# Layer-zero product at the head of the turn, and halves of the squares exchanged by transfers inside SBUF

## What is computed

```
x = _layernorm(x + _L0_gnn_ref(x, adj, L0_gnn_bias))     # similarity graph over the 512 columns
x = _layernorm(x + _L1_gnn_ref(x, adj, W_lang, W_grav, W_V, W_O, gate_logit, log_sigma))
x = _layernorm(x + _L2_gnn_ref(x, adj, L2_gnn_bias))     # similarity graph again
x = _layernorm(x + _L3_gnn_ref(x, adj, adj, L3_gnn_bias))
```

## Time and profile before

| what | value |
|---|---|
| time, median of 3 runs | 1690.02 us (1685.96 to 1690.75) |
| profiled execution: its own time | 1692.68 us |
| profiled execution: its span | 1690.8 us |
| TensorE busy | 1510.8 us, 89% |
| VectorE busy | 1245.2 us, 74% |
| ScalarE busy | 993.8 us, 59% |
| GpSimd busy | 637.9 us, 38% |
| `gnn_layer_pair` within the span | from about 318 to 1181 us |

### The profile page before, as it was taken

How to read it: one execution, slowest core, us unless ns; L and a number is a source line. 1 busy time by engine, 2 the same in 40 slices (tenths; PEclk the granted TensorE clock), 3 DMA queues, 4 the chain that set the end, 5 groups by cost and what they waited for, 6 DMA issues and landing times. The chain is left out here.

```text
span 1690.8 us, 27935 instructions
## 1 busy us (share of the span) xinstructions
PE 1510.8 (89%) x7672; PEld 1239.3 (73%) x7672; DVE 1245.2 (74%) x3177; ACT 993.8 (59%) x1715; POOL 637.9 (38%) x814
## 2 busy tenths in 40 slices
PE   6899999599999999999999999983799881999997
PEld 4677887487878887878877878862688881777774
DVE  5788799547776667776667776653677898699997
ACT  7775455236656666557666557654333780577775
POOL 5553001013234443334443334433000000799997
PEclk9999999699999999999999999996899995899998
DMA  5320493212111222112221112000541000344442
GB/s 213 103 85 1 176 379 143 87 51 70 62 38 61 68 75 68 56 37 68 68 75 68 44 50 68 31 26 26 205 144 57 0 0 0 119 149 140 146 143 106
DMA packets 80627, 148.19 MB, mean 88 GB/s; under 512 B 8448, under 2 KB 8576, under 8 KB 80576
## 3 DMA queue, kind: packets, MB, share of 16 engines
q1 hardware_dynamic: 80576, 147.56, 25.4%
HBM read 97.06 MB, written 50.46 MB: 87 GB/s over the span
## 5 line engine op out<-in xcount | busy, mean ns | idle before, releaser
L814 POOL TENSOR_TENSOR rs_a<-ve_a,neghalf 128x1 f32<-128x1 f32 x64 | 35.6, 556 | 375.1 <-DVE nm_a L808 375.1
L226 PE MATMUL bank<-xn_lo,xn_hi 128*128 128x512 f32 (+1 forms) x640 | 145.3, 358 | 5.3 <-DVE xn_lo L203 5.1
L198 ACT ACTIVATE xn_hi<-xn 128x512 fp32r<-128x512 f32 x128 | 80.6, 630 | 117.3 <-DVE xn L191 117.2
L1710 POOL TENSOR_TENSOR xw_lo<-xres,xw_hi 128x512 fp32r<-128x512 f32 x64 | 83.1, 1299 | 131.6 <-ACT xw_hi L1675 131.6
L226 PEld LDWEIGHTS bank<-xn_lo,xn_hi 128*128 128x128 f32 x640 | 102.5, 192 | 19.3 <-DVE xn_lo L203 10.3
L1649 PE MATMUL l_ps<-an_hi,xw_hi 128*128 128x512 f32 x256 | 105.6, 413 | 10.0 <-POOL xw_lo L1710 8.7
L217 PEld LDWEIGHTS bank<-xn_hi 128*128 128x128 f32 x512 | 95.7, 192 | 24.4 <-ACT xn_hi L198 7.7
L322 POOL TENSOR_TENSOR sq_lo<-sq,sq_hi 128x512 fp32r<-128x512 f32 x64 | 87.3, 1382 | 60.9 <-ACT sq_hi L289 60.8
L959 PE MATMUL l_ps<-an_hi,xw_hi 128*128 128x512 f32 x256 | 102.2, 399 | 8.8 <-DVE xw_lo L1340 8.4
L536 DVE MATCH_REPLACE8 work<-best,work 128x520 f32<-128x520 f32 x160 | 108.3, 684 | 0.0
L203 DVE TENSOR_TENSOR xn_lo<-xn,xn_hi 128x512 fp32r<-128x512 f32 x128 | 105.8, 827 | 0.6 <-ACT xn_hi L198 0.4
(11 more groups left out here) (242 smaller groups left out, 4742.1 us busy)
## 6 DMA issues: line engine op xcount, KB each, us to landing
xr<-in_x SPq DMA_DIRECT2D x32, 512.0 KB, 3.3
xw_dram<-stage SPq DMA_DIRECT2D x64, 256.0 KB, 5.6
stage<-xw_dram SPq DMA_DIRECT2D x64, 256.0 KB, 2.6
stage<-in_x SPq DMA_DIRECT2D x64, 256.0 KB, 2.6
between<-xo SPq DMA_DIRECT2D x64, 256.0 KB, 2.0
xres<-between SPq DMA_DIRECT2D x32, 512.0 KB, 3.7
xin<-between SPq DMA_DIRECT2D x64, 256.0 KB, 2.7
out<-xo SPq DMA_DIRECT2D x64, 256.0 KB, 2.0
```

What stands on the lines that cost most here:

```text
L226: mm = self.nc.tensor.matmul(out, h[:, c * P:(c + 1) * P], l[:, a:b], start=(i == 0 and c != 1), stop=False, skip_group_check=True)
L1710: nc.gpsimd.tensor_tensor(xw_lo[:, i % 2, :], of_batch(ga, i), xw_hi[:, i % 2, :].bitcast(F32), ALU.subtract).then_inc(xw_lo_ok, 1)
```

## The change

TensorE begins a turn with `l0(0)` and does `yprod(0)` after it; `l0(1)` comes directly behind `k_turned`, and `yprod(1)` between the pairs of `l1`. So that `l0(0)` can start, `xw_hi_(0)` and `xw_lo_(0)` of the following group are made at the end of the turn in front (ACT: behind `exp_g`; DVE: behind `kernel_g`, ahead of `ht_lo(3)`). `turns` passes the following group to each engine, and one more turn at the end is written out, so that the loop has 13 passes in place of 14. ACT scales the first kernel matrix in place of DVE; the small coefficient operations are put together. ACT no longer writes `sq_turned`: SP copies the two halves of `sq` by two transfers for each batch, eight in a turn, and POOL's `fold(i)` waits for them. ACT's `high(2)` and `high(3)` move behind `scale_l`, and POOL's order is another one.

```
+            def exchange(gp, i):
+                sp.wait_ge(sq_ok, GRP * gp + i + 1)
+                sp.dma_start(sq_turned[0:HALF, i, :], sq[HALF:P, i, :]).then_inc(exchanged[i], 16)
+                sp.dma_start(sq_turned[HALF:P, i, :], sq[0:HALF, i, :]).then_inc(exchanged[i], 16)
...
-                                ("store", 2), ("store", 3), ("load", 1), ("load", 2), ("next", 1), ("load", 3)):
+                                ("swap", 0), ("swap", 1), ("store", 2), ("store", 3), ("load", 1), ("load", 2),
+                                ("next", 1), ("load", 3), ("swap", 2), ("swap", 3)):
...
+                if A:
+                    l0(0)
                 if B:
                     yprod(0)
-                if A:
-                    l0(0)
                 if C:
                     k_turned()
-                if B:
-                    yprod(1)
+                if A:
+                    l0(1)
                 if C:
                     l1(0)
                     l1(1)
-                if A:
-                    l0(1)
+                if B:
+                    yprod(1)
...
+                def kernel_l_scaled():
+                    act.wait_ge(cf_ok, gp + 1)
+                    for i in range(GRP):
+                        nc.scalar.activation(k_l[:, i, :], k_l[:, i, :], ACT.Identity,
+                                             scale=small[:, 4, i:i + 1]).then_inc(ka_ok, 1)
...
-                    nc.scalar.activation(sq[:, i, :], xo[:, i, :], ACT.Square)
-                    nc.scalar.activation(sq_turned[0:HALF, i, :], xo[HALF:P, i, :], ACT.Square)
-                    nc.scalar.activation(sq_turned[HALF:P, i, :], xo[0:HALF, i, :], ACT.Square).then_inc(sq_ok, 1)
+                    nc.scalar.activation(sq[:, i, :], xo[:, i, :], ACT.Square).then_inc(sq_ok, 1)
...
                 if C:
-                    for i in range(GRP):
-                        high(i)
+                    high(0)
+                    high(1)
...
                     scale_l()
+                if C:
+                    high(2)
+                    high(3)
+                if B:
                     v_hi(2)
                 if A:
                     ht_hi(2)
                 if B:
                     exp_g()
+                if following is not None:
+                    xw_hi_(0, following)
...
                 def fold(i):
-                    pool.wait_ge(sq_ok, GRP * gp + i + 1)
+                    pool.wait_ge(exchanged[i], 32 * (gp + 1))
...
                 keep(2)
+                keep(3)
+                root_a(3)
                 if gp is not None:
                     fold(2)
                     fold(3)
-                keep(3)
-                if gp is not None:
                     sq_lo(0)
                     sq_lo(1)
-                root_a(3)
+                if g is not None:
+                    pool.wait_ge(q_ok, g + 1)
+                    nc.gpsimd.tensor_tensor(r_l[:], q_l[:], s.neghalf[:], ALU.pow).then_inc(r_ok, 1)
                 if gp is not None:
                     sq_lo(2)
                     sq_lo(3)
-                if g is not None:
-                    pool.wait_ge(q_ok, g + 1)
-                    nc.gpsimd.tensor_tensor(r_l[:], q_l[:], s.neghalf[:], ALU.pow).then_inc(r_ok, 1)
...
                     kernel_l()
                     kernel_g()
+                if following is not None:
+                    xw_lo_(0, following)
                 if A:
                     ht_lo(3)
```

More of the change, by code:

```diff
@@ L875, in gnn_layer_pair @@
         stored = [sem(f"stored{i}") for i in range(GRP)]
+        exchanged = [sem(f"exchanged{i}") for i in range(GRP)]
         passed = sem("passed")
@@ L879, in turns @@
         def turns(eng, turn):
[L881 to L886, removed]
+            turn(None, None, 0, 1)
+            turn(None, 0, 1, 2)
+            with eng.Fori(0, groups - 3) as gp:
+                turn(gp, gp + 1, gp + 2, gp + 3)
+            turn(groups - 3, groups - 2, groups - 1, None)
+            turn(groups - 2, groups - 1, None, None)
+            turn(groups - 1, None, None, None)
         @block.sync
@@ L918, in turn @@
                         store(at, i)
+                    elif kind == "swap" and gp is not None:
+                        exchange(gp, i)
                 if gp is not None:
@@ L935, in _, with turn @@
         def _(pe):
-            def turn(gp, g, ga):
+            def turn(gp, g, ga, following):
                 def hturn(i):
@@ L1209, in turn @@
                     y_hi(1)
+                if A:
+                    xw_hi_(2)
                 if C:
@@ L1213, in turn @@
                 if A:
-                    xw_hi_(2)
                     norm_a(0)
+                if B:
+                    y_hi(2)
                 if C:
@@ L1218, in turn @@
                     square(1)
+                if A:
+                    xw_hi_(3)
+                if C:
                     norm_b(2)
                     norm_b(3)
-                if B:
-                    y_hi(2)
                 if A:
                     norm_a(1)
+                if B:
+                    y_hi(3)
                 if C:
@@ L1345, in ht_lo, with xw_lo_ @@
                     lo_part(ht[1][:, :, i, :], ht_ps[i % 2][:].rearrange("p (c n) -> p c n", c=CH), ht[0][:, :, i, :], ht_lo_ok)
-                def xw_lo_(i):
+                def xw_lo_(i, ga=ga):
                     dve.wait_ge(xw_hi_ok, GRP * ga + i + 1)
@@ L1427, in kernel_l_scaled @@
                                                    in1=small[:, 2, :], op0=ALU.mult, op1=ALU.mult).then_inc(cf_ok, 1)
[L1428 to L1431, removed]
+                    nc.vector.tensor_scalar(small[:, 5, :], small[:, 3, :], s.w_g[:, 0:1], None, ALU.mult).then_inc(sg_ok, 1)
                 def kernel_sum():
[L1435 to L1442, removed]
+                    dve.wait_ge(sg_ok, gp + 1)
                     for i in range(GRP):
@@ L1478, in turn @@
                         ht_lo(i)
+                    xw_lo_(0, following)
                     return
+                if C:
+                    coefficients()
                 if A:
-                    xw_lo_(0)
+                    xw_lo_(1)
                 if C:
-                    kernel_l_scaled()
                     kernel_sum()
+                if A:
+                    residual_a(0)
                 if B:
                     y_lo(0)
-                if A:
-                    residual_a(0)
-                    xw_lo_(1)
                 if C:
@@ L1498, in turn @@
                     residual_b(1)
-                    stats_b(0)
-                    stats_b(1)
                 if A:
                     residual_a(1)
+                if B:
+                    y_lo(1)
                 if C:
@@ L1507, in turn @@
                     xw_lo_(2)
+                if C:
+                    stats_b(0)
+                    stats_b(1)
+                if B:
+                    y_lo(2)
+                if A:
+                    xw_lo_(3)
                     stats_a(1)
@@ L1516, in turn @@
                     stats_a(2)
-                    xw_lo_(3)
                 if B:
```

25 lines of the change are left out of this document (9 added, 16 removed).

## The result

The changed kernel takes 1723.78 us (median of four runs, 1721.78 to 1724.5) against 1688.8 beside it: a ratio of 1.021, 95% interval 1.019 to 1.022. The forecast was 1716.0 within 1688 to 1728. The profiled execution has a span of 1721.5 us, 30.7 more than before. From `k_turned` of turn 2 to that of turn 16, in TensorE's timeline, the 14 full turns take 745.45 us against 713.73: +31.7, all of the loss.

The account below looks back on a forecast made before the run. TensorE was taken as the bound, busy 49.86 of 51.0 us a turn. Fourteen turns at +1.91 (26.7) and edges -0.7 gave +26.0 on the profiled 1692.7, or 1718.7; on the median 1716.0, range 1688 to 1728.

Parts of the forecast that it names:

- The collision: VectorE's diagonals, two SBUF operands, wait for GpSimd's running fold and squares; end 2.55 us later, turn 1.91 longer.
- The exchange's landing: Second half issued at offset 33.4, landing at 35.4 to 36.0; fold(2) taken to start at 35.8.
- the collision with turns taken: Main case: diagonals and GpSimd operations alternate on the shared port; 1708 to 1724 us, chance 0.50.
- the exchange lands late: Rival: each microsecond fold(2) comes later lengthens the turn by one; 1730 us, chance 0.10 together with a lower clock.
- The clock: TensorE's clock may fall behind the 2 us wait in hturn(2); late exchange or lower clock, chance 0.10.
- the third rival: Exchange lands late or TensorE's clock falls; one such microsecond makes +14, 1730 us; chance 0.10.
- `k_turned`: TensorE's wait there goes, as coefficient, scalings and sums end by 3.6 us, before 4.2: 0.79 us a turn gained.
- the prediction counts three: Last three diagonals beside GpSimd's r_l: the port rule would cost about 0.7 us a turn; forecast that they pass.
- The edges: Turns outside the full ones: turn 1 +1.2, turn 2's start -0.6, turn 16 -2.2, turn 17 +0.9; sum -0.7 us.
- No collision, 1678.3: Rival: diagonals don't wait for GpSimd, or only briefly; a turn gains 0.64, total 1678.3 us; chance 0.18.
- The 0.75 for `high(2)` and `high(3)`: Placed behind scale_l on ScalarE, they start v_hi(2) 0.75 us later, all of it reaching the head of the turn.
- This alone is worth nothing: Removing ScalarE's eight second squares, 0.63 us each a turn, gains nothing in a full turn; TensorE's work covers them.

Follow-up runs that it names:

- m_from_psum: Changed kernel, with the eight diagonals on VectorE reading m from its PSUM bank, only the identity from SBUF: 1691.94 us, 1.002 of the kernel before.
- before_two_dummies: Kernel before, plus two 128x512 additions of constants on GpSimd ahead of r_l in turns 2 to 16, starting with the diagonals: 1715.76 us, 1.016.
- m_psum_high_late: Changed kernel, diagonals reading m from PSUM and ScalarE's high(2), high(3) moved from ahead of v_hi(2) to behind ht_hi(2): 1682.03 us, 0.996 of before.

## Why the prediction was right, point by point

*The collision* was right in place, mechanism and price: one wait for each GpSimd operation, the sides taking turns, 1.1 us a wait; two runs show it with nothing else changed, *m_from_psum* (-32 us) and *before_two_dummies* (+27 us). *The exchange's landing* was mis-sized: 35.8 was taken for `fold(2)`, 638.21 - 601.50 = 36.7 came, as issues took 0.47 to 0.60 and not 0.45, and the landing 2.9 and not about 2.4. So the first diagonal waits for nearly all of `fold(3)`: three waits, not two, an end at offset 43.1 for 42.7, and a turn of +2.37 for +1.91. In the 12 turns 3 to 14 that is 5.5 us, about the 5 by which the full turns exceed the sum (31.7 for 26.7). The other two are not like them: from `k_turned` to `k_turned` turn 2 lost 3.07 and turn 15 only 0.16. Turn 15 has no load in front of the exchange: its `swap(2)` is issued at offset 30.5 in place of 32.6, `fold(2)` starts at 34.2, and one diagonal waits. So 1723.78 is the upper end of the 1708 to 1724 given to the collision with turns taken, and a part of the rival *the exchange lands late* came with it: the range held, the forecast of 1716.0 was 8 us short.

*The clock* fell behind most of the waits in `hturn(2)`, as the third rival had it, but TensorE's slow matmuls took the place of a wait for VectorE. *`k_turned`* is reached without a wait, as said. Only two diagonals start behind `r_l` in the turn shown (644.12 and 644.35), where the prediction counts three; neither waited. *The edges*: turn 1, with the earlier start of turn 2, +0.4 for 1.2 - 0.6 (71.24 against 70.83 from the stage's first matmul to the first of turn 2); turn 16 -2.0 for -2.2 (48.31 against 50.34 from its first matmul to the next turn's), its 2.52 gone; turn 17 +2.3 for +0.9 (25.52 against 23.20 from `k_turned` to `squares`), the exchange having no cover.

*No collision, 1678.3*: this rival's size was wrong by 14 us (*m_from_psum*, 1691.94, turn 51.26 for 50.38). Its turn left out two waits. `r_l` comes behind `sq_lo(1)`: in the turn shown it ends at offset 42.75, and `scale_l` starts 0.44 later than `a_l` would have let it. With `fold(2)` at 35.8, as forecast, `r_l` would have been in time (42.75 - 0.9, an estimate), so this is the mis-sized landing again. `q_l`'s wait beside the row was not in the sum at all. The turn with the first wait alone took 50.88; how the mean's 0.88 divides between the two was not measured by an edit. The 0.75 for `high(2)` and `high(3)` was right (0.73).

*"This alone is worth nothing"*, of ScalarE's second squares, fell: in the new order, without the collision, they cost 1.44 us a turn. The work named as cover, TensorE's, does not cover them, as `v_hi(0)` and `m_out` stand behind them, and with `m_out` begins the chain for whose end TensorE waits. Under the collision it hardly showed (53.66 against 53.43): the diagonals began 2.1 us later and waited once in place of three times, and ended at the same offset.

## What to carry to other kernels

Before moving work on GpSimd, list what VectorE runs in the new window: operations with two SBUF operands, and some with one, can stand still for up to a whole GpSimd operation of 1.27 us each, so that a 0.3 us operation costs 1.3. (Beside the 128x4 `r_l` they did not.) Reading one operand from PSUM, or putting a dependency between the GpSimd operations so that they keep away, cost nothing here and gave back 29 to 32 of the 35 us. When such a delay is taken out, price again what stood behind it: the gains of an exchange and of an order depend on what else is late, and here each showed only when the next was mended.

## What the runs showed of the hardware

A VectorE operation with a single SBUF source can wait too: `q_l` (a 128x4 `tensor_scalar`, 0.16 us alone) took up to 1.30, and the 128x512 clamp of `a_g`, 0.43 alone, took in *m_psum_high_late* (min/median/max):

```profile
L1429 DVE TENSOR_SCALAR a_g<-a_g x16: 429/842/956, 383.5 to 1133.9; 128x512 f32<-128x512 f32 x16
```

The Trainium skill ("SBUF — State Buffer", section "SBUF: two separate sides") has the shared port taken by VectorE operations in a two-port mode as well as by those with two SBUF inputs; the two `tensor_scalar` rows agree, though no row shows the mode, and so does the diagonal with its operand from PSUM, which never waited. Its lock for the whole instruction does not describe `r_l`: a diagonal beside it took 0.30 in the changed kernel. And a transfer of half the partitions onto the other half inside SBUF, 128 KB, took 2.9 us from issue to landing, as long as a load of 256 KB from memory (2.8).
